# Fewer key tiles of maxima ahead of the scores, and modulation gates computed in halves, in a two-layer AdaLN network

## What is computed

```python
mod = (_silu(L0_c) @ L0_wmod).reshape(L0_c.shape[0], 6, 1, -1)
sa, ca, ga, sb, cb, gb = (mod[:, 0], ..., mod[:, 5])
ga = (2 * (ga >= 0) - 1) * jnp.maximum(jnp.abs(ga), 0.25)
h = _layernorm(x, axis=-1) * (1 + ca) + sa
x = x + ga * _L0_attn_ref(h, ...)
h = _layernorm(x, axis=-1) * (1 + cb) + sb
x = x + gb * _L0_ffn_ref(h, ...)
```

```python
attn = jnp.einsum('bqhd,bkhd->bhqk', q, k) / jnp.sqrt(jnp.asarray(hd, x.dtype))
attn = jax.nn.softmax(attn, axis=-1)
attn_out = jnp.einsum('bhqk,bkhd->bqhd', attn, v).reshape(B, S, D)
```

## Time and profile before

| what | value |
|---|---|
| runs | 3407.12, 3410.4, 3411.89 us (median 3410.4) |
| profiled execution | 3405.77 us, its span 3404.0 us |
| PE busy | 3235.8 us, 95% |
| DVE busy | 2773.8 us, 81% |
| ACT busy | 2645.6 us, 78% |
| POOL busy | 632.3 us, 19% |
| DMA | 242.40 MB |

### The profile page before, as it was taken

How to read it: one execution, slowest core, us unless ns; L and a number is a source line. 1 busy time by engine, 2 the same in 40 slices (tenths; PEclk the granted TensorE clock), 3 DMA queues, 4 the chain that set the end, 5 groups by cost and what they waited for, 6 DMA issues and landing times. The chain is left out here.

```text
span 3404.0 us, 69251 instructions
## 1 busy us (share of the span) xinstructions
PE 3235.8 (95%) x25649; PEld 1631.2 (48%) x25650; DVE 2773.8 (81%) x5189; ACT 2645.6 (78%) x4676; POOL 632.3 (19%) x649
## 2 busy tenths in 40 slices
PE   8999999999999999788999888999999999999997
PEld 5444444444444443577777656644444444444442
DVE  8889999999999996453777666299999999999991
ACT  3179999999999999433333223699999999999996
POOL 5520000000000000053321163133333210000001
PEclk9789999999999999889999998999999999999999
DMA  8642321202022100445100376613131331202001
GB/s 279 183 116 70 47 37 22 44 20 42 16 47 37 22 15 7 135 157 166 35 28 13 131 242 207 159 35 59 38 58 32 61 64 38 45 18 42 15 16 49
DMA packets 312713, 242.40 MB, mean 71 GB/s; under 512 B 206743, under 2 KB 258872, under 8 KB 307730
## 3 DMA queue, kind: packets, MB, share of 16 engines
q1 hardware_dynamic: 296068, 188.89, 23.7%
q0 software_dynamic: 14832, 47.79, 4.3%
q10 hardware_dynamic: 1504, 1.64, 0.1%
HBM read 129.63 MB, written 109.05 MB: 70 GB/s over the span
## 5 line engine op out<-in xcount | busy, mean ns | idle before, releaser
L1075 DVE TENSOR_REDUCE att_in_part_max<-att_l_prod_ps 128x1 f32<-128x512 f32 (+1 forms) x2440 | 1816.4, 790 | 149.9 <-PE att_l_prod_ps L951 143.6
L1025 ACT ACTIVATE att_l_probs<-att_l_prod_ps 128x512 f32<-128x512 f32 x3072 | 1724.0, 606 | 82.6 <-PE att_l_prod_ps L972 30.6
L987 PE MATMUL att_l_o_ps<-att_l_probs,att_l_v_sb 128*17 128x288 f32 (+2 forms) x12288 | 1183.9, 457 | 15.5 <-ACT att_l_probs L1025 13.9
L972 PE MATMUL att_l_prod_ps<-att_in_q_sb,att_in_k_sb 50*128 50x512 f32 x2048 | 671.6, 449 | 9.1 <-DVE att_l_o_ps L1093 9.1
L972 PE MATMUL att_l_prod_ps<-att_in_q_sb,att_l_k_sb 50*128 50x512 f32 x2048 | 655.2, 449 | 1.7 <-DVE att_in_part_max L1075 1.7
L951 PE MATMUL att_l_prod_ps<-att_l_k_sb,att_in_q_sb 50*128 50x512 f32 x1792 | 551.9, 432 | 0.0
L1033 ACT ACTIVATE att_l_probs<-att_l_prod_ps 128x1024 f32<-128x1024 f32 x512 | 521.5, 1018 | 0.0
L951 PE MATMUL att_l_prod_ps<-att_in_k_sb,att_in_q_sb 50*128 50x512 f32 x1624 | 504.7, 436 | 0.0
L972 PEld LDWEIGHTS att_l_prod_ps<-att_in_q_sb,att_in_k_sb 50*128 50x128 f32 x2048 | 311.8, 185 | 246.8 <-ACT att_l_probs L1025 120.7
L987 PEld LDWEIGHTS att_l_o_ps<-att_l_probs,att_l_v_sb 128*17 128x17 f32 x12288 | 205.5, 95 | 462.7 <-issue 249.5
L972 PEld LDWEIGHTS att_l_prod_ps<-att_in_q_sb,att_l_k_sb 50*128 50x128 f32 x2048 | 301.3, 184 | 260.4 <-ACT att_l_probs L1025 155.0
(11 more groups left out here) (284 smaller groups left out, 3294.7 us busy)
## 6 DMA issues: line engine op xcount, KB each, us to landing
att_in_q_sb<-q_hi SPq DMA_DIRECT2D x256, 64.0 KB
slot_rows<-att_l_zeros POOLq DMA_DIRECT2D x10, 1024.0 KB, 4.4
ffn_parts<-slot_rows SPq DMA_DIRECT2D x40, 256.0 KB, 3.1
tile_out<-ffn_parts SPq DMA_DIRECT2D x40, 256.0 KB, 2.2
att_in_q_sb<-q_lo SPq DMA_DIRECT2D x128, 72.0 KB
att_l_v_sb<-v_rows SPq DMA_DIRECT2D x16, 544.0 KB, 15.8
att_in_k_sb<-k_hi SPq DMA_DIRECT2D x32, 256.0 KB, 9.3
att_l_k_sb<-k_hi SPq DMA_DIRECT2D x32, 256.0 KB, 9.4
```

Of the source, the lines that this page charges most:

```text
L972: nc.tensor.matmul(prod_ps[:, BANK_OF[f"s{c}"]], k_sb[j // GPB % 2][rows, pair, u * P:(u + 1) * P], q_sb[rows, j % QR, pair], start=True, ...
L987: last = nc.tensor.matmul(o_ps[32 * h:32 * h + AUG, c0:c1], v_sb[:, j // GPB % 2, u, h * AUG:(h + 1) * AUG], probs[:, (n * KT + u) % PB, h ...
L1025: nc.scalar.activation(probs[:, (n * KT + u) % PB, c % HG], prod_ps[:, BANK_OF[f"s{c}"]], ACT.Exp, scale=float(HD) ** -0.5).then_inc(exp_d ...
L1075: nc.vector.reduce_max(dst, prod_ps[:, bank:bank + len(units)], AX.X).then_inc(units_taken, 1)
```

## The change

`LEAD` goes from 8 to 4: maxima run four key tiles ahead. `FIRST` becomes 40, the units of step n+1 are complete after w=5, the row maxima are taken at w = (16 - 4) // 2 = 6, and the last 10 periods of a loop have no maxima. The DMAs of `store_shift` stay one store and four loads.

The gates are computed in halves of 128 columns, 16 calls for each layer in place of 8, and in the same units as the columns: layer 0's columns beside units 0 to 7 and its half gates beside units 0 to 15, layer 1's columns and half gates beside units 22 to 37. The experts' items whose unit is gone are run after the first maxima. `store_result` waits in addition for the stores of the result before.

```diff
-LEAD = 8
+LEAD = 4
...
-                if k in (MOD_AT[0] + 10, MOD_AT[1] + 25):
+                if k in (MOD_AT[0] + 10, MOD_AT[1] + 17):
...
-            def gates(layer, v, b, kh):
-                o, c0, k = (v * B + b) * D, (2, 5)[v] * D, (layer * KH + kh) * B + b
-                return nc.tensor.matmul(gate_rows[:, o:o + D], cs[:, k:k + 1].broadcast_to([P, P]), wmod[:, kh, c0:c0 + D],
+            def gates(layer, i):
+                v, b, part, kh = i // 8, i // 4 % 2, i // 2 % 2, i % 2
+                o, c0, k = (v * B + b) * D + part * P, (2, 5)[v] * D + part * P, (layer * KH + kh) * B + b
+                return nc.tensor.matmul(gate_rows[:, o:o + P], cs[:, k:k + 1].broadcast_to([P, P]), wmod[:, kh, c0:c0 + P],
                                         start=(kh == 0), stop=(kh == KH - 1))
...
-                elif 8 <= i < 16:
-                    last = gates(0, (i - 8) // 4, i // 2 % 2, i % 2)
+                if 0 <= i < 16:
+                    last = gates(0, i)
                     if i == 15:
                         last.then_inc(rows_ready, 1)
...
-                if 0 <= i < 8:
-                    last = gates(1, i // 4, i // 2 % 2, i % 2)
-                    if i == 7:
+                if 0 <= i < 16:
+                    last = columns(cols[:, 1, i // 4, i // 2 % 2], 1, i // 4, i // 2 % 2, i % 2)
+                    if i == 15:
+                        last.then_inc(cols_done, 1)
+                    last = gates(1, i)
+                    if i == 15:
                         last.then_inc(rows_ready, 1)
-                elif 8 <= i < 24:
-                    last = columns(cols[:, 1, (i - 8) // 4, i // 2 % 2], 1, (i - 8) // 4, i // 2 % 2, i % 2)
-                    if i == 23:
-                        last.then_inc(cols_done, 1)
...
-RESULT_STEP, ROWMAX_STEP = 1, LEAD // STEP_TILES
+RESULT_STEP, ROWMAX_STEP = 1, (KT - LEAD) // STEP_TILES
...
             eng.wait_ge(o_ready, n + 1)
+            if n > 0:
+                eng.wait_ge(o_stored, n * 16 * HG)
...
-                                dve.wait_ge(units_taken, period_of(n, LEAD // STEP_TILES) * len(TAKES))
+                                dve.wait_ge(units_taken, period_of(n, ROWMAX_STEP) * len(TAKES))
...
             first_maxima(nc, pe, ai, qk_ps, beside)
+            for i in range((FIRST - MAX_FIRST + 1) // 2, ITEMS_B):
+                item(i)
             turn_item(ITEMS_B)
```

## The result

The changed kernel takes 3487.9 us in the median of four runs (3482.1 to 3493.2), the kernel before 3411.1: a ratio of 1.0229, 95% interval 1.0217 to 1.0242, slower by 77. The forecast was 3457, slower by 47, with a range that ended at 3485. Sign and mechanism were right, the size was not.

The account below looks back on a forecast made before the run. PE and ACT, busy without a gap in the attention loops, were taken to bound the kernel, any PE wait paid in full. +43 - 3.2 + 0.4 - 3.6 + 10 = +46.6 on 3410.4 gave 3457 us, range 3412 to 3485.

Parts of the forecast that it names:

- Part 1: Attention loops: the shift-row chain starts two periods later, so PE waits 0.33 to 0.75 us at each quiet boundary; +43 us.
- the term of +43: Both attention loops: 60 boundaries at 0.72 us each for late shift rows, bounds +24 and 56.
- 0.4: Ends of both attention loops: two more periods with maxima per layer, +0.2 us a layer.
- a boundary that costs more than its wait: Sign for the loops: ACT and PE take periods to find their pace again, making Part 1 too small; no size given.
- The late group of layer 1: Layer 1's loop: the stop from DVE's transpose waiting 1.92 us more for POOL goes away, -3.2 us.
- Part 3: Layer 0's first maxima and modulations: later gate rows leave POOL's gate chain uncovered; +10 us, bounds +4 and +17.
- the +12 of the working: Layer 0's stage: the loop begins at 201.4 us instead of 189.4, before allowing for units at full clock.
- R2: Rival: the clock stays up in layer 0's maxima and POOL is covered, -6.4 instead of +10, 3441 us; chance 0.05.
- Part 2: Layer 1's first maxima: eight units leave the stretch before the loop, four pairs of them beside expert items; -3.6 us.
- R1: Rival: shift rows land in time, within 7.88 us of the row maximum, so Part 1's 43 is gone; 3414 us, chance 0.14.
- the main case: Whole kernel: all terms together give 3457 us, 3433 to 3480 with the bounds of all terms; chance 0.76.
- R3: Rival: slow landings are common beside the next step's query loads, 1.0 to 1.3 us a boundary, 3474 to 3492; chance 0.05.

## Why the prediction was right and wrong

**Part 1, the chain: mechanism right, price too low.** PE waits at each of the 60 boundaries that carry maxima, with a median of 0.63, and a quiet one makes its period about 0.68 longer, in the upper half of the 0.33 to 0.75 worked out; about 0.07 is won back in the period behind it. The step that failed is the term of +43, 60 x 0.72: it cut down the lateness that its own rows gave, and it took a stop to cost its length. The two loops grew by 74.6 in the traces, where the prediction's terms for them, 43 - 3.2 + 0.4, make 40. Of these two errors the second is half of the gap of 34:

- The landings of the trace of before, walked one by one, summed to 55 of overdraft. Measured were 58.3. The prediction had nearly the right number in hand and cut it to 43, for that part of layer 1's extras "which are past at w=6" and for what would be won back. Of layer 1's extras before, 3.0 were two stores issued late, by 2.0 and 1.0, and these are indeed gone in the changed kernel; but 8.7 were slow hops, and of those the changed kernel has 8.2, at other steps (the store's hop took 3.51, 2.49 and 2.84 before the third to fifth steps). What is won back, 0.07 in 60 periods, is 4.5. Of the gap this is 58.3 - 4.5 - 43 = 11.
- A stop was priced at its length. Of the 11 boundaries of the changed kernel whose period was longest (1.55 to 4.93 over the usual) nine were followed by 1.4 or more of extra time, of the other 49 none by more than 0.24; together 18.4. The prediction named "a boundary that costs more than its wait" as what would make Part 1 too small, but put it down to ACT and PE finding their pace, not to the clock, and gave it no price.

That price stood in the trace of before. The prediction took from the earlier trace rows that a transpose 1.92 late cost its step 3.2, and read from it only that a stop isn't made up, not why 3.2 is more than 1.9. PE's row in that place, and the two parts of the period, the first with the stop, the second behind it:

```profile
2364.33 0.49 PE L972 MATMUL att_l_prod_ps<-att_in_q_sb,att_l_k_sb 50*128 50x512 f32 x1 [1.70 <-DVE att_in_part_max L1075]
```

```profile
2361.90:2366.00 4.10, 2.40 (x20) 0.88 (x18) 2.51 (x6) 2.60 (x5) 3.88 (x5) 1.00 0.14 17
2366.00:2369.87 3.87, 3.87 (x26) 1.10 (x24) 2.88 (x5) 2.69 (x5) 1.83 (x1) 0.56 0.04 9
```

PE stood for 1.70, and then the granted clock was 0.56: the stop cost 1.7 and the half clock behind it most of the rest of 3.3 (the period is 7.97 long, others 4.65).

Of the 5 that remain, 4 lie in the periods which the waits end: they are longer than usual by 62.6 in all, not by 58.3. The last 1 is not told apart.

**The late group of layer 1, -3.2: right.** With four and six tiles ahead and no other stops layer 1's loop takes 1193.0 to 1194.8, 2.7 to 4.5 under the 1197.5 of before, and the period that was 7.97 long is 4.64 in the changed kernel. The size is that of one execution: with eight tiles and half gates the same period costs 1.3 and the loop 1195.8.

**Part 3, layer 0's stage, +10: mechanism right, the size partly by luck.** POOL's chain is what the loop now waits for, and its 15.4 stood as worked out. The loop began 9.3 later, by errors that cancel. A half gate call measures 0.70 to 0.73, not 0.83, so a unit takes 1.87 and not 2.07, and from the first maxima to the copy of the gates passed 61.2, not 65.5: 4.3 less than in the +12 of the working. Against it, 1.2 came ahead of the first maxima (their start lies between 118.6 and 121.7 in the twelve traces), and from POOL's end to the first score passed 2.7, not 1.5. That 1.5 ends at the window's start of 189.40; the first score of before came at 190.10, 2.3 behind DVE's end. The 2 taken off for a clock that might stay up had no part in it: from 124 on the clock was at half, and R2 didn't come. (In the earlier trace rows the clock until 123 is 1.00; the 0.84 that the prediction read is the DMA share.)

**Part 2, layer 1's first maxima, -3.6: measured -1.2**, where the items account for -2.9 (118.0 from the first turn of rows to the last, before 121.0); the wait for the first expert rows was 8.7 instead of 7.0 in this execution and took 1.7 of it back. Over all traces the items bear the forecast out: 121.0 to 121.4 with 48 units (three kernels), 118.8 to 120.4 with 44 (three), 116.9 to 118.8 with 40 (six), the first and the last 3.6 apart in the mean. The whole stretch, 150.7 to 156.5, varies more, since that wait lies between 4.4 and 8.7.

**R1** fell by the margin that was given: the chain took 8.56 against 7.88. (With the bounds of all terms added up, the main case lies at 3431 to 3482, not at 3433 to 3480; the result is outside of both.) **R3**, late hops made common, didn't come: hops over 2 us were 14 of 64, before 11. That the result lies at R3's time (3474 to 3492) is luck: the late ones were about as many as before, and cost 2 to 8 each for a reason that R3 didn't have.

## What to carry to other kernels

Where a chain of transfers has slack, count it in the slowest landings of the trace and not in the median one, and add up the overdraft as it stands; shaving it by hand cost this forecast 11 of the 34 that it fell short. A full engine pays for a stop twice if its clock falls behind it: look in the rows of before for a stop that cost more than its length, and ask why. When a helper step is moved (here gates behind columns), look for the engine that starts from its end, since its chain, not the moved work, can set the stage.

## What the runs showed of the hardware

Stops of TensorE of under 2 us were often followed by matmuls at half clock although the engine had been full before. With six loads PE stands for 1.81 to 4.90 at every boundary: behind 36 stops of under 2 us 25 times about another 1.4 or more was lost, behind the 24 longer ones 23 times, 4.3 to 5.6 in six cases. In the changed kernel stops of 1.48 and 1.49 were followed by it and others of 1.61 and 1.86 were not, so no length parts the two. In the other direction, a PE without a gap did not get its clock back in layer 0's first maxima; the changed kernel's windows there show 10.00 busy of 10.00 at 0.50 twice, from 155 to 175, and before 15.00 of 15.00:

```profile
155.00:165.00 10.00, 10.00 (x33) 6.34 (x32) 6.32 (x6) 0.00 (x0) 5.00 (x2) 0.50 0.00 0
165.00:175.00 10.00, 10.00 (x35) 6.60 (x33) 6.76 (x8) 0.00 (x0) 0.00 (x0) 0.50 0.00 0
```

Why the clock stays low there and comes back within one or two periods in the loop, these runs don't show; no run tried it. The issue of one load of a shift row costs SP 0.69 (2.75 for four); with four of the six transfers half a row long, six took 3.99, so half the data saved little. Two loads of two rows that are contiguous in DRAM take 0.54 together, but the store that arranges them so takes 0.53 to issue in place of 0.34, and its hop 1.95 in place of 1.44 (medians; the last rows of the experiments show one such pair).
